# Splitting six PSUM score banks 4 and 2 instead of 3 and 3 in a causal attention stage

## What is computed

```
qkv = x @ w_qkv                      # 16 heads of size 8
q = q * cos + rotate_half(q) * sin   # the same for k
att = q @ k.T * 8 ** -0.5
att = where(causal, att, most negative float)
y = softmax(att) @ v
x = x + y @ w_proj
```

## Time and profile before

| | us |
|---|---|
| three runs | 749.75, 750.62, 919.63 |
| median | 750.62 |
| span of the profiled execution, first to last instruction | 748.4 |
| causal stage in it, steps 0 to 7 | 316.9 to 621.1, that is 304.2 |

### The profile page before, as it was taken

One profiled execution on the slowest core, in us unless ns is written; L12 is line 12 of the kernel. 1 busy time (PEld: TensorE's weight loads), 2 busy tenths in 40 slices (PEclk: granted clock), 3 DMA queues, 4 the chain that ended last, 5 costly groups with the idle time before them and its releaser, 6 DMA issues.

```text
span 748.4 us, 11770 instructions
## 1 busy us (share of the span) xinstructions
PE 666.3 (89%) x4108; PEld 456.7 (61%) x4108; DVE 501.7 (67%) x1560; ACT 356.8 (48%) x728; POOL 159.1 (21%) x290
## 2 busy tenths in 40 slices
PE   1875767899997997799998899999999997999998
PEld 1664656677776775465555555565555545777775
DVE  3578874776676648977665667769877425666654
ACT  3744355212222464166677678665666673222221
POOL 4563544330002430002433420203020000000000
PEclk9999989989999996799999999999999999999999
DMA  8000000000000000000000000000000000000000
GB/s 293 2 0 1 1 0 1 2 1 1 0 1 1 0 2 1 0 1 1 1 2 1 1 2 1 1 1 2 1 1 2 1 1 1 1 15 1 15 15 14
DMA packets 5722, 7.27 MB, mean 10 GB/s; under 512 B 416, under 2 KB 4640, under 8 KB 5664
## 3 DMA queue, kind: packets, MB, share of 16 engines
q1 hardware_dynamic: 4944, 4.59, 1.9%
q10 hardware_dynamic: 720, 1.93, 0.8%
HBM read 5.47 MB, written 1.05 MB: 9 GB/s over the span
## 4 chain that ended last, share of the span: by engine, by line
PE 70%; DVE 11%; ACT 4%; issue 3%; POOL 2%; POOLq 0%; ACTq 0%; DVEq 0%
PE bank L1568 12%; PE bank L1466 10%; PE bank L1596 10%; PE bank L1526 9%; PE bank L1251 6%; PE bank L1253 5%; PE bank L1252 5%; PE bank L1449 3%; PE bank L1578 2%; DVE hn L862 2%; DVE bank L1134 1%; DVE work L1137 1%; PE bank L1536 1%; PE bank L1259 1%; PE bank L1507 1%
## 5 line engine op out<-in xcount | busy, mean ns | idle before, releaser
L771 ACT ACTIVATE arena<-bank 128x512 f32<-128x512 f32 (+3 forms) x384 | 167.1, 493 | 88.7 <-PE bank L1578 65.1
L1134 DVE CUSTOM_DVE_ANT_0 bank<-bank,mask_qk 128x512 f32<-128x512 f32 (+3 forms) x256 | 121.2, 511 | 48.6 <-PE bank L1596 47.7
L1596 PE MATMUL bank<-kza,qta 128*128 128x512 f32 (+3 forms) x320 | 127.0, 410 | 5.7 <-DVE work L1134 2.0
L698 ACT ACTIVATE work<-bank 128x512 f32<-128x512 f32 x80 | 47.6, 597 | 171.7 <-PE bank L1449 171.7
L1568 PE MATMUL bank<-qtb,kza 128*128 128x512 f32 (+3 forms) x320 | 120.3, 388 | 2.0 <-ACT arena L771 1.0
L1061 DVE TENSOR_TENSOR work<-work,bank 128x512 f32<-128x512 f32 x80 | 54.9, 687 | 82.7 <-ACT work L698 82.2
L1137 DVE TENSOR_REDUCE work<-bank 128x1 f32<-128x512 f32 x128 | 81.6, 684 | 24.4 <-PE bank L1596 23.7
L1568 PEld LDWEIGHTS bank<-qtb,kza 128*128 128x128 f32 x320 | 60.5, 192 | 57.8 <-ACT arena L771 52.1
L1466 PE MATMUL bank<-dw,work 128*128 128x128 f32 x640 | 92.0, 288 | 0.1
L1466 PEld LDWEIGHTS bank<-dw,work 128*128 128x128 f32 x640 | 79.5, 195 | 11.5 <-issue 10.4
L1526 PE MATMUL bank<-arena 128*9 128x512 f32 (+3 forms) x768 | 80.1, 489 | 0.4 <-ACT arena L771 0.4
(11 more groups left out here) (200 smaller groups left out, 1166.0 us busy)
## 6 DMA issues: line engine op xcount, KB each, us to landing
x<-x_in SPq DMA_DIRECT2D x4, 256.0 KB, 10.1
y_out<-x SPq DMA_DIRECT2D x4, 256.0 KB, 2.3
arena<-const_in ACTq DMA_DIRECT2D x1, 976.0 KB, 8.0
arena<-gw_in SPq DMA_DIRECT2D x1, 640.0 KB, 9.2
arena<-uw_in SPq DMA_DIRECT2D x1, 640.0 KB, 8.4
dw<-dw_in SPq DMA_DIRECT2D x1, 640.0 KB, 9.4
work<-q_in SPq DMA_DIRECT2D x2, 256.0 KB, 6.9
arena<-wa_in ACTq DMA_DIRECT2D x1, 393.0 KB, 8.5
```

What stands on the lines that cost most here:

```text
L771: act.activation(pb[:, blk % 2, h, 0:w], s_bank(n)[:, 0:w], ACT.Exp, scale=SCALE).then_inc(p_ready, 1)
L1134: ins = dve.tensor_tensor_reduce(out=src, in0=src, in1=mask_qk[:, CW - w:], scale=1.0, scalar=-3e38, op0=ALU.add, op1=ALU.max, accum_out=dst)
L1596: pe.matmul(a_bank(n)[:, 0:w], qta[:, slot(b, g), i * P:(i + 1) * P], kz(s, h, half)[:, 0:w], start=True, stop=True).then_inc(a_full, 1)
```

## The change

Of the six score banks four go to the transposed scores and two to the scores for the maxima. In `s_bank` the rotation becomes `bank[1 + n % 4]` (banks 1 to 4), in `a_bank` it becomes `bank[5 + n % 2]` (banks 5 and 6) from step 0 on. The wait of score n is for the exp of slot n - 4 instead of n - 3, the wait of max n for the drain of slot n - 2 instead of n - 3. Nothing else changes: no instruction is added, removed or moved.

```
-S_DEEP, A_DEEP = 3, 3
+S_DEEP, A_DEEP = 4, 2
```

## The result

| | before | after |
|---|---|---|
| median of the runs, us | 753.57 (4 runs; 750.62 at the time of the prediction) | 780.35 (4 runs, 777.05 to 784.2) |
| span of the profiled execution, us | 748.4 | 775.5 |
| ratio | | 1.0362, 95% interval 1.0296 to 1.0427 |

One of the four runs before, 919.63 us, was slow; the ratio compares the other three (median 750.62) with the four after. Forecast were 785.0 us with a range of 773 to 796, a ratio of 1.046. The sign and the mechanism hold; the loss is smaller than forecast. In the two profiled executions the span grew by 27.1 us where the sum had 34.4.

What follows compares the result with a forecast made beforehand. TensorE's in-order queue was taken to set the time of steps 0 to 6. 748.4 + 36.0 (max waits) - 1.6 (score waits) = 782.8 span; runs' median 2.2 above it: 785.0 us, range 773 to 796.

Steps and rivals of the forecast that it cites:

- the sum: On the profiled execution's span: 748.4 us plus 36.0 lost in steps 0 to 6 minus 1.6 gained in step 7, 782.8.
- The wait of max 2 for drain 0: Steps 0 to 6: max 2 waits for drain 0 of its own block; 0.36 us lost in plain block 6, step 6.
- the twelve of the forecast: Losses forecast for the 12 blocks of step 6, from 0.12 to 0.96 us each, sum 5.2 us.
- the 0.11 us for a late load: After a late load the next matmul follows after 0.34 us instead of 0.23: 0.11 more, if not late before.
- The score side: Score n waits for exp n - 4: 0 gained in steps 0 to 6, 1.6 us in step 7 (blocks 1, 6, 7, 9).
- every block loses again: Steps 0 to 6: nothing gives a block's loss back, VectorE's average slack does not help; sum 36.0 us.
- a bound of 3 us in step 4: Lower bound: VectorE's backlog in step 4 counted once instead of per block takes another 3 us off, giving 24.
- the bound of 42 us: Upper bound of the loss: 0.11 us per late load also at masked blocks, 8 blocks in 7 steps, 6 us more.
- (a): Rival: only large waits count, blocks 1 and 5 and three blocks of step 4 lose; 765 us, chance 0.08.
- (b): Rival: TensorE's clock falls to step 2's 0.96 in all of steps 0 to 6; 795 us, chance 0.08.
- (c): Rival: loads bound the kernel, a fourth bank lets score 3 load during the sums; 739.8 us, chance 0.02.
- (d): Rival: neither side matters, VectorE frees a bank within 0.92 us from max 0 to max 2; 750 us, chance 0.04.

Runs made afterwards that it cites:

- e1: Kernel before, three banks each, but max n waits for drain n - 2 as after the change: 781.83 us, ratio 1.0429.
- e2: Kernel before, three banks each up to step 6, four score banks in step 7 only: 751.15 us, ratio 0.9972.
- e4: Changed kernel (four and two banks) with maxima spread out: score 0, score 1, max 0, score 2, max 1, sums, max 2, score 3, max 3: 755.54 us, ratio 1.0057.
- e11: Kernel before, three banks each and four score banks in step 7, with VectorE's negate moved behind drain 0 of blocks 1 and 5: 752.08 us, ratio 0.999.
- e8: Kernel before, three banks each, but max n waits for drain n - 1, just ahead of it: 955.47 us in one run.
- e7: Mirror image of the change, against the kernel before: two banks for the transposed scores, four for the maxima: 820.96 us, ratio 1.093.

## Why the prediction was right, and where it was off

**The wait of max 2 for drain 0: right in place and in size, where nothing else moved.** In step 6 the losses after the change were 0.11, 0.95, 0.19, 0.30, 0.36, 0.56, 0.35, 0.50, 0.12, 0.45, 0.38, 0.30, sum 4.6, against the twelve of the forecast with sum 5.2. Eight of the twelve agree within 0.02. The load 0.05 us behind the drain that frees its bank and the 0.11 us for a late load are in the rows after, each loss lengthens its block, and e1 shows that it is the wait alone.

**The score side: right but for 0.4 us.** In step 7 1.2 us were gained (1.6 forecast, block 1 counted in error). In steps 0 to 6 the term was put at 0 and is 0.4, in block 11 of steps 1 and 2 and block 3 of step 2 (e2). Idle load time behind the sums is no stall: it hardly moved when a bank was added (57.8 to 54.7) and moved to another line when the order changed (e4).

**The failing step: "every block loses again", with drain 0 at a fixed distance from the start of its block.** It holds where drain 3 waits only for max 3. It fails where VectorE is behind with work of its own, for then the loss of one block gives VectorE time to catch up, and the next block loses less. In block 4 `yout` stands between the drains, and `negate` follows them, so VectorE works without a pause from drain 0 of block 4 to drain 0 of block 5. Before, drain 0 of block 4 and score 0 of block 5 (its drain 0 is in the earlier trace rows):

```profile
565.70 0.69 DVE L1137 TENSOR_REDUCE work<-bank 128x1 f32<-128x512 f32 x1 [0.56 <-PE bank L1596]
...
567.42 0.40 PE L1568 MATMUL bank<-qtb,kza 128*128 128x512 f32 x1
```

The same after, with `negate` and drain 0 of block 5:

```profile
591.02 0.69 DVE L1137 TENSOR_REDUCE work<-bank 128x1 f32<-128x512 f32 x1 [0.57 <-PE bank L1596]
...
593.10 0.39 PE L1568 MATMUL bank<-qtb,kza 128*128 128x512 f32 x1
...
593.91 0.17 DVE L1168 TENSOR_SCALAR stm<-work 128x16 fp32r<-128x16 f32 x1
594.12 0.19 DVE L1169 SCALAR_TENSOR_TENSOR stm<-work,stm 128x16 fp32r<-128x16 f32 x1
594.23 1.97 DVE L1137 TENSOR_REDUCE work<-bank 128x1 f32<-128x512 f32 x3
...
594.96 0.19 PEld L1596 LDWEIGHTS bank<-kza,qta 128*128 128x128 f32 x1 [0.61 <-DVE work L1137]
```

VectorE's stretch is as long as it was: 565.70 to 569.59 and 591.02 to 594.91, 3.89 us both. Block 4 grew by 0.36 around it, so drain 0 of block 5 ends 1.81 us after score 0 where it ended 2.17 after it. So block 5 lost 0.56 and not 0.91, in four steps of seven; in step 4 block 9 lost 0.26 and not 0.65, block 11 0.82 and not 1.39, and in step 5 block 1 lost 1.65 and not 1.98, where VectorE is behind too; there the path was not followed row by row. The measured terms by step are 4.6, 2.8, 0.8, 4.0, 6.6, 5.3, 4.6, sum 28.6 before rounding, against 5.0, 3.6, 3.3, 4.5, 8.1, 6.3, 5.2, sum 36.0. Of the 7.4 us between, block 5 makes 2.0 over the seven steps, the three blocks of steps 4 and 5 make 1.3, and step 2 has 1.4 of another kind, below. I had named this backlog as a bound of 3 us in step 4 and not looked for it in block 5, where it recurs in every step. The 0.07 to 0.09 us too much in blocks 3, 10 and 11, the narrow ones where max 1 holds up first, is a smaller error of the same sum. So is the range's upper end: by the bound of 42 us it would be 748.4 + 42 - 1.6 + 2.2 = 791, well inside the 796 that is said to hold it only nearly.

**Step 2 was compared with a stretch of low clock.** Of its missing 2.5 us 1.4 are in block 0. Before, in the first 6.3 us of step 2, the busy times by stretch read

```profile
394.70:401.00 6.30, 5.26 (x27) 2.87 (x26) 2.91 (x9) 3.55 (x7) 0.10 (x1) 0.73 0.01 3
```

and after

```profile
401.80:408.00 6.20, 5.14 (x34) 3.14 (x32) 3.96 (x16) 4.56 (x10) 0.51 (x3) 1.00 0.01 3
```

The granted clock was 0.73 there and is 1.00 now. Both stretches hold the same wait of 1.0 us for a key tile from ScalarE. It is not the split of the banks: of the kernels with three banks each in this step, e2 has the dip (step 2 as long as before, 46.7 us) and e11 has not (45.2). The same stretch in e2, then in e11:

```profile
395.70:402.00 6.30, 5.26 (x27) 2.90 (x26) 2.90 (x9) 3.55 (x7) 0.10 (x1) 0.73 0.01 3
```

```profile
397.10:403.30 6.20, 5.16 (x37) 3.15 (x35) 3.92 (x14) 4.67 (x10) 0.65 (x3) 1.00 0.01 3
```

Against a profile of before without the dip the loss would thus be some 1.4 us more than the 27.1. What sets off the dip stays open.

**The rivals.** (a), only large waits count, falls: blocks with 0.35 us of wait lose 0.35. (b), the clock, did not come true at this dose (1.00 in steps 1 to 7, 0.95 in step 0 where it was 0.94 before) but did at the next one, in e8. The Trainium skill, "TensorE: Matmul & The Clock Gate", section "A second HAM failure mode: psum-queue depth-cycling", describes a clock that goes back and forth between its levels because TensorE idles briefly between groups of matmuls again and again. e8 agrees, with 1.00 in one block 0 and 0.50 in another; the changed kernel, with matmuls at 37.68 of 39.45 us in step 6, stayed at 1.00 there. (c) falls, since score 3's load still starts as the sums end (0.86 us of idle time ahead of it as before), and (d), since max 2 does wait.

## What to carry to other kernels

How many buffers a pair of engines needs is not read from how busy the reader is but from the longest burst that the writer issues. With two banks the third matmul of a burst costs the time from the start of the first to its drain (1.12 us here), less the distance that it had to the first (0.92), plus 0.05 for the release and 0.11 for the late load: 0.36 us, in every burst, though VectorE was idle a fifth of the time. ScalarE, idle almost half, was outrun just so (e7). Before giving a bank away, list for each block when the buffer would be free and when it is wanted; and before writing that difference down for every block, ask whether the reader's lateness was set by the writer or by its own queue, for in the second case one wait pays for part of the next. The order of the queue was worth nearly as much as the bank: of the 27.4 us that the stage had grown by, some 23.5 came back by spreading the burst (e4).

## What the runs showed of the hardware beyond that

A load of weights released late costs 0.11 us more than the wait itself where no small matmul stands ahead of it: the next matmul follows 0.34 us after it in place of 0.23, before, and in e7 for the score loads too. With the maxima held to one at a time (e8), the granted clock fell to 0.80 over 478 us, with matmuls counted as busy for 382.54 of 478.35 us; in step 6 after the change it was 1.00, with 37.68 of 39.45. And profiles of kernels with the same order and the same banks in step 2 differ there by 1.4 us through one dip of the clock, so that a difference of that size in one block needs its clock row beside it.
